# Rewriting the attention stage of a six-stage kernel: its norm inside, query tiles in another order, first maxima beside the projections, products over half rows

## The chip, the cores and the metric

The kernel is one program on one core of a Trainium2 chip. The metric is device time in microseconds (us), the median of several runs of the whole program. Engines are named as in the profile: PE is the TensorE matmul, PEld its weight load, DVE is VectorE, ACT is ScalarE, POOL is GpSimd, SP is the queue that issues the transfers.

## What is computed

Six stages run one after the other on `x` (2 sequences of 512 tokens, width 512), each on a layer norm of `x`: a feed-forward with 4-bit weights, a Mamba-2 block, the same feed-forward again, a routed low-rank block, causal attention, the routed block again.

```python
x = x + 0.5 * _L0_ffn_ref(_layernorm(x), ...)
x = x + _L0_attn_ref(_layernorm(x), ...)
x = x + 0.5 * _L0_ffn_ref(_layernorm(x), ...)
x = x + 0.5 * _L1_ffn_ref(_layernorm(x), ...)
x = x + _L1_attn_ref(_layernorm(x), L1_attn_Wq, L1_attn_Wk, L1_attn_Wv, L1_attn_Wo)
x = x + 0.5 * _L1_ffn_ref(_layernorm(x), ...)
```

The attention has 32 query heads and 8 key heads of size 16; q and k are rotated by cos and sin:

```python
q = _apply_rope(q, cos, sin)
k = jnp.repeat(_apply_rope(k, cos, sin), GROUPS, axis=1)
logits = jnp.where(causal, jnp.einsum('bhqd,bhkd->bhqk', q, k) * scale, lowest)
attn = jax.nn.softmax(logits, axis=-1)
out = jnp.einsum('bhqk,bhkd->bhqd', attn, v)
return out.transpose(0, 2, 1, 3).reshape(bsz, q_len, NH * HD) @ Wo.T
```

## The kernel before

Each stage is a function that writes its own instruction lists, one per engine (`@block.tensor`, `@block.vector` and so on), which run in the order written and wait for each other on semaphores. Between stages all engines meet at a barrier (`Chip.leave`, L52 and L53). PSUM has eight banks of 512 columns, `ps[0]` to `ps[7]`.

The attention stage (`attention`, L830) first calls `norm_transpose` (L100), which makes the normalised, transposed `hT` behind a barrier of its own, while the weights are loaded. Then, for each of the two sequences (b), `project(b, i)` makes nine products: i=0 is k, 1 to 4 are q, 5 to 8 are v. One step later `rotate(b, i-1)` multiplies by the rotation matrix and `rope` (DVE) combines, with ACT taking the high part (`high_part`) and DVE the low part. One step later again `place(b, i-2)` spreads the result over 8 (k) or 4 (q) stacks of 128 rows, each a pair of matmuls into bank `z % 4`, which ACT (even z) or DVE (odd z) copies out (`keep`, L1149 and L1218). A stack holds two heads, one in its upper and one in its lower 64 rows.

The softmax needs each row's maximum before the exponentials. A *step* is one query tile of 128 tokens of one sequence (`STEPS`, 8 of them, tiles 3, 2, 1, 0). `score(s, z)` is one *unit*: two heads' products of a query tile with all its keys, and two additions of the causal mask, into banks 0 and 1 or 2 and 3 by turns (L1020, L1023); `peak(s, z)` is DVE's maximum over it (L1225). 16 units make a step. `turn_maxima(s)` transposes the maxima (L1029), ACT and DVE split them in two parts, and `maxima(s)` on SP writes them by four transfers into spare rows of the stacks, so that the next products have them subtracted. The units of the first two steps stand alone, ahead of the loop; those of step s+2 stand inside step s.

The loop runs over 40 *quads* (step, half of the heads, key tile). In a quad `score_t` makes four transposed products (L1042, and L1044 for the mask on the diagonal) into banks 4 and 5, ACT takes the exponentials (L1162), and one quad later `weigh` multiplies them with v (L1055, four column groups of 32 at once, bank 6). After each half step `turn_out` and `normalize` (L1069, L1238, L1239), after each step `turn_normed`, `take_normed`, `out_product` and `add_out` (L1077, L1174, L1085, L1249) use bank 7.

Of the kernel before, what the change touches and what calls it, by code (L numbers as in the profile page):

```python
# [79 lines left out]

class Chain:
# [16 lines left out]


def norm_transpose(nc, g, name, dst, xn, rms_w=None, var_out=None, sync=None,  # L100
                   pool_end=None, act_start=None):


    x, ps, ident, nhalf = g["x"], g["ps"], g["ident"], g["nhalf"]
    with ExitStack() as ctx:
        c = Chip(nc, ctx, name)
        st = c.sb("st", [P, NT, 6])
        mv = c.sb("mv", [P, NT, 2])
        ve = c.sb("ve", [P, NT])
        rstd = c.sb("rstd", [P, NT])  # L110
        ss = c.sb("ss", [P, NT])
        sq = c.sb("sq", [P, 2, D])
        r2 = c.sb("r2", [P, NT])
        xr = c.sb("xr", [P, NT, D]) if rms_w is not None else xn
        paired = isinstance(dst, Pair)
        xw = c.sb("xw", [P, 2, DT, P]) if rms_w is not None else None
        var_ready, rstd_ready, xn_ready, ss_ready, r2_ready, xr_ready, t_done, t_used, dve, v2, hi_ready, \
            lo_ready = (c.sem(s) for s in ("var_ready", "rstd_ready", "xn_ready", "ss_ready", "r2_ready",
                                           "xr_ready", "t_done", "t_used", "dve", "v2", "hi_ready", "lo_ready"))

        def bank(t):
            return ps[t % 2].rearrange("p (a n) -> p a n", a=DT)

        def cols(t):
            return slice(t * P, (t + 1) * P)

        with nc.Block() as block:
            @block.sync
            def _(e):
                if sync is not None:  # L130
                    sync(e)

            @block.vector
            def _(e):
                ch = Chain(e, dve)
                for t in range(NT):
                    ch.step(e.bn_stats(st[:, t, :], x[:, t, :]))
                ch.wait()
                for t in range(NT):
                    ch.step(e.bn_aggr(mv[:, t, :], st[:, t, :]))  # L140
                ch.wait()
                e.tensor_scalar(ve[:], mv[:, :, 1], EPS, None, ALU.add).then_inc(var_ready, 1)
                e.wait_ge(rstd_ready, 1)
                for t in range(NT):
                    e.tensor_scalar(xn[:, t, :], x[:, t, :], mv[:, t, 0:1], rstd[:, t:t + 1],
                                    ALU.subtract, ALU.mult).then_inc(xn_ready, 1)
                if var_out is not None:
                    e.wait_ge(xn_ready, NT)
                    for t in range(NT):
                        ch.step(e.bn_stats(st[:, t, :], xn[:, t, :]))  # L150
                    ch.wait()
                    for t in range(NT):
                        ch.step(e.bn_aggr(mv[:, t, :], st[:, t, :]))
                    ch.wait()
                    ch.link(e.tensor_copy(var_out[:], mv[:, :, 1]))
                if rms_w is not None:
                    e.wait_ge(xn_ready, NT)
                    for t in range(NT):
                        ch.step(e.tensor_tensor(x[:, t, :], x[:, t, :], xn[:, t, :], ALU.add))
                    e.wait_ge(ss_ready, NT)  # L160
                    e.tensor_scalar(ve[:], ss[:], 1.0 / D, EPS, ALU.mult, ALU.add).then_inc(v2, 1)
                    e.wait_ge(r2_ready, 1)
                    for t in range(NT):
                        e.tensor_scalar(xr[:, t, :], xn[:, t, :], r2[:, t:t + 1], None,
                                        ALU.mult).then_inc(xr_ready, 1)
                    for t in range(NT):
                        e.wait_ge(t_done, t + 1)
                        if t >= 2:
                            e.wait_ge(lo_ready, t - 1)
                        w = rms_w[:, :].unsqueeze(2).to_broadcast([P, DT, P])  # L170
                        e.tensor_tensor(xw[:, t % 2], bank(t), w, ALU.mult).then_inc(t_used, 1)
                elif paired:
                    for t in range(NT):
                        e.wait_ge(hi_ready, t + 1)
                        e.tensor_tensor(dst.lo[:, :, cols(t)], bank(t), dst.hi_read[:, :, cols(t)],
                                        ALU.subtract).then_inc(t_used, 1)

            @block.gpsimd
            def _(e):
                e.wait_ge(var_ready, 1)  # L180
                e.tensor_tensor(rstd[:], ve[:], nhalf[:, 0:NT], ALU.pow).then_inc(rstd_ready, 1)
                if rms_w is not None:
                    e.wait_ge(v2, 1)
# [646 lines left out]
def attention(nc, g, name):  # L830
# [18 lines left out]
    with ExitStack() as ctx:  # L849
# [67 lines left out]
        def units_at(t):  # L917

            s, j, kt = QUADS[t]
            if s + 2 >= NS:  # L920
                return []
# [1406 lines left out]
```

## Time and profile before

| what | value |
|---|---|
| median of 3 runs | 2520.4 us (2519.33 to 2521.07) |
| the profiled execution | 2520.89 us, its span 2519.0 us |
| PE, DVE, ACT, POOL busy over the span | 94%, 66%, 52%, 53% |
| attention with its norm | 2098.9 to 2454.0 us of the span |
| of it the norm | 2098.9 to 2117.5 |
| projections of sequence 0, of sequence 1 | 2117.5 to 2158.4, 2158.4 to 2198 |
| the first two steps' maxima, alone | 2198 to 2238 |
| the loop over quads and its end | 2238 to 2454 |

The busy share is of instructions on an engine, and a busy PE need not be at its peak: its clock is granted at 1.2 or 2.4 GHz (0.5 or 1.0 in the profile), and the same matmuls take twice as long at the lower.

### The profile page before, as it was taken

What the parts mean: (1) busy time and instruction counts of PE and PEld (TensorE: products, weight loads), DVE (VectorE), ACT (ScalarE), POOL (GpSimd) and SP (SyncE); (2) the same over time, 40 slices, a digit from 0 to 9 for tenths busy, and PEclk for the clock granted to TensorE, in tenths of its full rate; (3) what the DMA queues carried; (4) which work ended last, traced back from release to release, by engine and by line L of the source; (5) the groups of instructions that cost most, each with busy time, mean ns of one, the idle gap of its engine ahead of it and who ended that gap; (6) DMA issues with size and microseconds to landing.
All of it is one profiled execution on the core that took longest, in us unless ns stands there. A gap on an engine that the chain in (4) does not pass through costs nothing. (4 is left out here: it accounts for less than half of the span.)

```text
span 2519.0 us, 32506 instructions
## 1 busy us (share of the span) xinstructions
PE 2371.8 (94%) x12122; PEld 1833.6 (73%) x12122; DVE 1661.3 (66%) x2163; ACT 1313.1 (52%) x1902; POOL 1329.8 (53%) x875
## 2 busy tenths in 40 slices
PE   6997899999999999999999999999889986989986
PEld 5876688888888888888888888888668753565643
DVE  5555887687588588588578678678365535674424
ACT  2323576477477467467467567567423223325533
POOL 2221498599499499589579679669622200000000
PEclk9998999999999999999999999999889998989997
DMA  4321333233233233233233323323134202000001
GB/s 128 97 80 46 115 110 105 89 96 119 79 111 115 80 104 103 93 100 114 88 102 109 92 89 117 98 95 102 46 84 97 90 14 78 1 2 2 2 1 47
DMA packets 163260, 203.98 MB, mean 81 GB/s; under 512 B 24380, under 2 KB 86080, under 8 KB 162976
## 3 DMA queue, kind: packets, MB, share of 16 engines
q1 hardware_dynamic: 163104, 201.90, 26.3%
q8 instruction: 98, 1.61, 0.2%
q14 instruction: 58, 0.48, 0.1%
HBM read 198.37 MB, written 3.15 MB: 80 GB/s over the span
## 5 line engine op out<-in xcount | busy, mean ns | idle before, releaser
L1892 POOL TENSOR_TENSOR mamba_w_lo<-mamba_raw,mamba_w_hi 128x512 fp32r<-128x512 f32 x272 | 436.1, 1613 | 289.9 <-ACT mamba_w_hi L1720 289.9
L76 PE MATMUL psum<-mamba_hT_lo,mamba_w_hi 128*128 128x512 f32 x1152 | 461.7, 401 | 5.6 <-DVE mamba_bc L1983 3.0
L77 PE MATMUL psum<-mamba_hT_hi,mamba_w_hi 128*128 128x512 f32 x1152 | 456.2, 396 | 0.0
L78 PE MATMUL psum<-mamba_hT_hi,mamba_w_lo 128*128 128x512 f32 x1152 | 456.1, 396 | 0.0
L1911 POOL TENSOR_SCALAR mamba_L<-mamba_A,mamba_ts 128x256 f32<-128x256 f32 (+1 forms) x256 | 334.3, 1320 | 0.1
L2015 DVE TENSOR_TENSOR mamba_L<-mamba_L,mamba_cb 128x1536 f32<-128x1536 f32 x128 | 302.0, 2359 | 22.2 <-ACT mamba_L L1769 16.5
L76 PEld LDWEIGHTS psum<-mamba_hT_lo,mamba_w_hi 128*128 128x128 f32 x1152 | 217.0, 188 | 55.9 <-DVE mamba_bc L1983 3.3
L1983 DVE SCALAR_TENSOR_TENSOR mamba_hid<-psum,mamba_cw,mamba_hid 128x1022 f32<-128x1022 f32 (+2 forms) x192 | 245.1, 1277 | 18.0 <-ACT mamba_hid L1727 13.5
L78 PEld LDWEIGHTS psum<-mamba_hT_hi,mamba_w_lo 128*128 128x128 f32 x1152 | 216.9, 188 | 52.4
L77 PEld LDWEIGHTS psum<-mamba_hT_hi,mamba_w_hi 128*128 128x128 f32 x1152 | 216.9, 188 | 49.1
L2042 DVE SCALAR_TENSOR_TENSOR mamba_zs_lo<-mamba_z,mamba_dgn,mamba_zs_hi 128x512 fp32r<-128x512 f32 x128 | 117.6, 923 | 172.0 <-ACT mamba_zs_hi L1792 172.0
L395 POOL TENSOR_TENSOR ffn_w_lo<-ffn_deq,ffn_w_hi 128x512 fp32r<-128x512 f32 (+2 forms) x66 | 86.2, 1307 | 262.6 <-ACT ffn_w_hi L405 262.6
L2000 DVE SCALAR_TENSOR_TENSOR mamba_L<-mamba_A,mamba_ts,mamba_zero 128x256 f32<-128x256 f32 (+1 forms) x512 | 214.7, 487 | 1.1 <-DMA mamba_A<-mamba_a_dram 1.1
L76 PE MATMUL psum<-mamba_w_lo,mamba_zs_hi 128*128 128x512 f32 x512 | 205.7, 402 | 10.0 <-DVE mamba_zs_lo L2042 10.0
L78 PE MATMUL psum<-mamba_w_hi,mamba_zs_lo 128*128 128x512 f32 x512 | 203.0, 396 | 0.0
L77 PE MATMUL psum<-mamba_w_hi,mamba_zs_hi 128*128 128x512 f32 x512 | 203.0, 396 | 0.0
L1792 ACT ACTIVATE mamba_zs_hi<-mamba_z,mamba_dgn 128x512 fp32r<-128x512 f32 x128 | 91.7, 722 | 200.2 <-PE psum L78 200.2
L566 POOL MEMSET routed_qT<- 1x1024 f32 x2 | 1.9, 945 | 356.5 <-POOLq L53 356.5
L1727 ACT ACTIVATE mamba_hid<-psum,mamba_cw 128x1024 f32<-128x1024 f32 x64 | 77.3, 1208 | 201.0 <-PE psum L78 201.0
L1720 ACT CAST mamba_w_hi<-mamba_raw 128x512 fp32r<-128x512 f32 x272 | 165.7, 610 | 27.2 <-PE psum L78 25.8
L1574 PE MATMUL psum<-mamba_L,mamba_hc 128*64 128x256 f32 x1024 | 159.4, 390 | 3.6 <-DVE mamba_L L2015 3.6
L2028 DVE SCALAR_TENSOR_TENSOR mamba_z<-mamba_hid,mamba_dgn,psum 128x1024 f32<-128x1024 f32 x64 | 81.9, 1280 | 120.2 <-PE psum L1578 120.2
(278 smaller groups left out, 5002.7 us busy)
## 6 DMA issues: line engine op xcount, KB each, us to landing
mamba_A<-mamba_a_dram SPq DMA_DIRECT2D x128, 512.0 KB, 4.4
mamba_raw<-in_win SPq DMA_DIRECT2D x144, 256.0 KB, 2.6
mamba_raw<-in_wout SPq DMA_DIRECT2D x128, 256.0 KB, 2.6
mamba_Eb<-mamba_e_dram SPq DMA_DIRECT2D x128, 128.0 KB, 3.0
ffn_raw<-in_w SPq DMA_DIRECT2D x80, 128.0 KB, 3.5
ffn_scl<-in_s SPq DMA_DIRECT2D x80, 128.0 KB, 3.7
ffn_scl<-in_s SPq DMA_DIRECT2D x86, 64.0 KB, 2.3
ffn_raw<-in_w SPq DMA_DIRECT2D x20, 256.0 KB, 2.6
```

Source lines behind the costliest of these rows:

```text
L76: e.matmul(out, wh, ml, start=start, stop=False)
L77: e.matmul(out, wh, mh, start=False, stop=False)
L78: return e.matmul(out, wl, mh, start=False, stop=stop)
L1574: e.matmul(psum[lo:lo + HD, 5 + b, q:q + HALF], hc[:, token_tile(b, c, 0), lo:lo + HD], L[:, m % 3, c, h, 0:HALF], start=True, stop=False)
L1720: e.copy(w.hi[:, k % NSPLIT, :], raw[:, k % NRAW, :]).then_inc(s["w_hi"], 1)
L1792: e.activation(zs.hi[:, q % 2, :], z[:, i, p, :], ACT.Copy, scale=dgn[:, grp, i, 1:2]).then_inc(s["z_hi"], 1)
L1892: e.tensor_tensor(w.lo[:, k % NSPLIT, :], raw[:, k % NRAW, :], w.hi_read[:, k % NSPLIT, :], ALU.subtract).then_inc(s["w_lo"], 1)
L1911: last = e.tensor_scalar(out, A[:, m % 2, h, lo:SEQ], ts[:, token_tile(b, 1, j), 1, head], 0.0, ALU.subtract, ALU.min)
L1983: ins = e.scalar_tensor_tensor(t[:, :, k:], banks(kind, n)[:, :, :SEQ - k], cw[:, grp, i, 3 - k:4 - k], t[:, :, k:], ALU.mult, ALU.add)
L2000: last = e.scalar_tensor_tensor(out, A[:, m % 2, h, lo:hi], ts[:, token_tile(b, c, j), 1, head], zero[:, 0:1].to_broadcast([P, hi - lo]), ...
L2015: e.tensor_tensor(t, t, cb[:, m % 2].unsqueeze(2).to_broadcast([P, 2, 2, WCOL]), ALU.mult).then_inc(s["m_ready"], 1)
L2042: e.scalar_tensor_tensor(zs.lo[:, q % 2, :], z[:, i, p, :], dgn[:, grp, i, 1:2], zs.hi_read[:, q % 2, :], ALU.mult, ALU.subtract).then_inc ...
```

## The change

Nearly all of it is in the attention stage.

- `norm_transpose` is gone. Statistics, normalisation and transposes stand in the attention's own lists: tiles 0 to 3, then `project(0, 0)`, then tiles 4 to 7. POOL converts `sel`.
- The steps take the query tiles 1, 2, 3, 0. Units of tile 1 hold two stacks (`DEEP` 2) and those of tile 0 four, so steps 0, 1, 6 and 7 have 8, 8, 4 and 4 units.
- `score` and `score_t` use 64 rows per head in place of 128 with zeros; the two heads of a stack use the two halves of the array. The mask is added from halves too: four matmuls a unit in place of two.
- `score` has banks 0 and 1 alone and waits for the unit before it (`peaked, k`; it was `peaked, k - 1`). `score_t` has banks 2 to 5.
- The eight units of step 0 and two of step 1 stand beside the projections of sequence 1 (`BESIDE`), whose stacks go through banks 2 and 3 alone (`stack_bank`). The other units stand in up to four slots of a quad (`WITHIN`, `SLOTS`): 3 to 4 a quad up to quad 15 (2 in quads 6 and 11), 2 in quads 16 to 25, 1 in 26 to 33.
- All stages get `keep_clock`: transposes of the identity whose result nobody reads, while PE would wait at the start of a stage. The feed-forward takes `hT` rows ahead of the first weights, and the routed block orders `query(1)`, `score(1)` and `pick` earlier.

```diff
+def keep_clock(e, out, ident, n):
+    for _ in range(n):
+        e.transpose(out[:, 0:P], ident[:], ident[:])
...
-    STEPS = [(b, qt) for qt in reversed(range(QT)) for b in range(SEQS)]
+    STEPS = [(b, qt) for qt in (1, 2, 3, 0) for b in range(SEQS)]
...
+    BESIDE = {0: {0: 2, 1: 2, 2: 2, 3: 1, 4: 1}, 1: {7: 1, 8: 1}}
+    WITHIN = {1: {0: 3, 1: 3}, 2: {1: 1, 2: 3, 3: 4, 4: 4, 5: 4}, 3: {6: 2, 7: 3, 8: 3, 9: 3, 10: 3, 11: 2},
...
+        def stack_bank(b, z):
+            return z % 4 if b == 0 else 2 + z % 2
...
                 def score(s, z):
                     b, qt = STEPS[s]
-                    k, n = s * NQ + z, P * (qt + 1)
-                    if k >= 2:
-                        e.wait_ge(peaked, k - 1)
-                    for h in range(2):
-                        e.matmul(psum[:, 2 * (k % 2) + h, 0:n], qs[:, b, z, qt * P:(qt + 1) * P],
-                                 ks[:, b, 2 * (z // QPK) + h, 0:n], start=True, stop=False)
-                    for h in range(2):
-                        last = e.matmul(psum[:, 2 * (k % 2) + h, n - P:n], identr[:], maskr[:], start=False, stop=True)
+                    k, n = UNIT[s, z], P * (qt + 1)
+                    if k:
+                        e.wait_ge(peaked, k)
+                    for y in range(DEEP[s]):
+                        for h in range(2):
+                            e.matmul(psum[:, h, y * n:(y + 1) * n], qs[HALVES[h], b, z + y, qt * P:(qt + 1) * P],
+                                     ks[HALVES[h], b, 2 * ((z + y) // QPK) + h, 0:n], start=y == 0, stop=False)
+                    for j in range(2):
+                        for h in range(2):
+                            out = psum[:, h, 0:DEEP[s] * n].rearrange("p (y n) -> p y n", y=DEEP[s])
+                            last = e.matmul(out[:, :, n - P:n], shifted[HALVES[h], P // 2 * (1 - j):P // 2 * (1 - j) + P],
+                                            halfm[HALVES[h], j, :].unsqueeze(1).to_broadcast([P // 2, DEEP[s], P]),
+                                            start=False, stop=j == 1)
                     last.then_inc(scored, 1)
...
+                for i in range(NV):
+                    ahead, behind = beside(i)
+                    for u in ahead:
+                        score(*u)
+                    project(1, i)
+                    if 1 <= i <= NR:
+                        rotate(1, i - 1)
+                    if 2 <= i <= NR + 1:
+                        place(1, i - 2, behind)
...
                 for t in range(TEND):
+                    if t < TQ:
+                        score_t(t, 0)
+                    for u in unit_in(t, 0):
+                        score(*u)
+                    if t in MAXIMA_AT:
+                        turn_maxima(MAXIMA_AT[t])
+                    if 1 <= t <= TQ:
+                        weigh(t - 1)
+                    for u in unit_in(t, 1):
+                        score(*u)
+                    if t < TQ:
+                        score_t(t, 1)
+                    for u in unit_in(t, 2):
+                        score(*u)
```

On PE, a quad off the diagonal in the first step of before holds two units (L1020 and L1023) between the transposed products (L1042), and then the product with v (L1055):

```order
L1042 MATMUL psum<-attn_qs,attn_ks 128x512 x2
L1020 MATMUL psum<-attn_ks,attn_qs 128x384 x2
L1023 MATMUL psum<-attn_maskr,attn_identr 128x128 x2
L1042 MATMUL psum<-attn_qs,attn_ks 128x512 x2
L1020 MATMUL psum<-attn_ks,attn_qs 128x384 x2
L1023 MATMUL psum<-attn_maskr,attn_identr 128x128 x2
L1055 MATMUL psum<-attn_hT,attn_v 32x512 x4
```

On PE in the changed kernel, the end of quad 3 and the most of quad 4 (L992 and L996 are the transposed products, L964 and L969 a unit, L1008 the product with v):

```order
L996 MATMUL psum<-attn_identr,attn_halfm 128x4x64 x4
L964 MATMUL psum<-attn_ks,attn_qs 128x384 x2
L969 MATMUL psum<-attn_halfm,attn_shifted 128x128 x4
L964 MATMUL psum<-attn_ks,attn_qs 128x384 x2
L969 MATMUL psum<-attn_halfm,attn_shifted 128x128 x4
L992 MATMUL psum<-attn_qs,attn_ks 128x512 x2
L964 MATMUL psum<-attn_ks,attn_qs 128x384 x2
L969 MATMUL psum<-attn_halfm,attn_shifted 128x128 x4
L1008 MATMUL psum<-attn_hT,attn_v 32x512 x4
L964 MATMUL psum<-attn_ks,attn_qs 128x384 x2
L969 MATMUL psum<-attn_halfm,attn_shifted 128x128 x4
L992 MATMUL psum<-attn_qs,attn_ks 128x512 x2
```

Four units stand in a quad where two did, each with four mask matmuls, and between two of them there is at most one other group.

On DVE in the changed kernel, the projections of sequence 1 from the first rope on (L1206 to L1211 are `rope`, L1217 `keep`, L1227 `peak`):

```order
L1206 TENSOR_TENSOR attn_early<-attn_early,attn_cos 128x512
L1208 TENSOR_TENSOR attn_early<-psum,attn_sin 128x512
L1209 TENSOR_TENSOR attn_early<-attn_early 128x512
L1211 TENSOR_TENSOR attn_parts_lo<-attn_early,attn_parts_hi 128x512
L1227 TENSOR_REDUCE attn_mx<-psum 128x2x2 x2
L1206 TENSOR_TENSOR attn_early<-attn_early,attn_cos 128x512
L1208 TENSOR_TENSOR attn_early<-psum,attn_sin 128x512
L1209 TENSOR_TENSOR attn_early<-attn_early 128x512
L1211 TENSOR_TENSOR attn_parts_lo<-attn_early,attn_parts_hi 128x512
L1217 CAST attn_ks<-psum 128x512
L1227 TENSOR_REDUCE attn_mx<-psum 128x2x2
L1217 CAST attn_ks<-psum 128x512 x3
```

Before, this stretch has no reduce: all of them come after the last copy of a stack. Now two stand behind the first rope and one between two copies.

## Rows read from the trace of the kernel before

**Rows 1.** The page: busy time of each engine, and the granted clock in 40 slices.

```profile
PE 2371.8 (94%) x12122; PEld 1833.6 (73%) x12122; DVE 1661.3 (66%) x2163; ACT 1313.1 (52%) x1902; POOL 1329.8 (53%) x875
...
PEclk9998999999999999999999999999889998989997
```

**Rows 2.** Windows: stretch, length, then busy us per engine, granted clock, DMA, GB/s.

```profile
2098.90:2117.50 18.60, 6.91 (x32) 5.41 (x32) 9.82 (x25) 7.64 (x11) 2.36 (x3) 0.63 0.75 262
...
2158.40:2198.00 39.60, 37.17 (x132) 21.86 (x130) 21.04 (x32) 13.40 (x27) 0.00 (x0) 1.00 0.01 1
2198.00:2238.00 40.00, 31.12 (x130) 23.60 (x131) 37.05 (x33) 0.26 (x1) 0.00 (x0) 0.91 0.01 1
2238.00:2454.00 216.00, 199.67 (x1095) 124.09 (x1095) 84.89 (x143) 104.54 (x191) 0.00 (x0) 0.97 0.01 2
```

**Rows 3.** Timeline of the units that stand alone: start us, length us, instruction.

```profile
2201.26 3.48 DVE L1225 TENSOR_REDUCE attn_mx<-psum 128x2 f32<-128x1024 f32 x3
...
2202.53 0.72 PE L1020 MATMUL psum<-attn_ks,attn_qs 128*128 128x512 f32 x2 [0.23 <-DVE attn_mx L1225]
...
2203.09 0.33 PE L1023 MATMUL psum<-attn_maskr,attn_identr 128*128 128x128 f32 x2
```

**Rows 4.** Timeline of one quad of the loop.

```profile
2262.68 0.42 PEld L1020 LDWEIGHTS psum<-attn_ks,attn_qs 128*128 128x128 f32 x2
2262.87 2.28 ACT L1162 ACTIVATE attn_hT<-psum 128x512 f32<-128x512 f32 x4 [1.34 <-PE psum L1042]
...
2263.63 0.96 DVE L1225 TENSOR_REDUCE attn_mx<-psum 128x2 f32<-128x768 f32 x1 [1.22 <-PE psum L1023]
...
2264.97 1.07 PE L1055 MATMUL psum<-attn_hT,attn_v 128*32 128x512 f32 x8
...
2265.96 0.19 PEld L1042 LDWEIGHTS psum<-attn_qs,attn_ks 128*128 128x128 f32 x1 [0.84 <-ACT attn_hT L1162]
```

**Rows 5.** Groups by shape from 2198 to 2454: busy us, mean ns, idle before.

```profile
L1162 ACT ACTIVATE attn_hT<-psum 128x512 f32<-128x512 f32 x160 | 89.3, 596 | 70.5 <-PE psum L1044 42.2 <-PE psum L1042 25.2
...
L1225 DVE TENSOR_REDUCE attn_mx<-psum 128x2 f32<-128x1024 f32 x32 | 36.8, 1218 | 3.6 <-PE psum L1023 3.4
L1085 PE MATMUL psum<-attn_wo,attn_oT 128*128 128x512 f32 x64 | 32.6, 657 | 0.8 <-ACT attn_oT L1174 0.8
L1225 DVE TENSOR_REDUCE attn_mx<-psum 128x2 f32<-128x768 f32 x32 | 30.7, 959 | 25.5 <-PE psum L1023 25.5
```

**Rows 6.** Timeline of `rotate` and `place` of k, sequence 1.

```profile
2169.53 1.02 PE L999 MATMUL psum<-attn_raw,attn_rot 128*128 128x512 f32 x2
...
2172.57 1.07 ACT L1149 CAST attn_ks<-psum 128x512 fp32r<-128x512 f32 x2
...
2173.31 1.28 DVE L1218 CAST attn_ks<-psum 128x512 fp32r<-128x512 f32 x2
...
2175.54 0.59 PE L986 MATMUL psum<-attn_hT,attn_wq 128*128 128x512 f32 x1
```

**Rows 7.** Transfers of the maxima from 2216 to 2245: KB, us to landing.

```profile
attn_qs<-attn_mh SPq DMA_DIRECT2D x4, 8.0 KB, 1.9
```

**Rows 8.** Timeline of a unit at the lower clock.

```profile
2218.50 0.55 PEld L1020 LDWEIGHTS psum<-attn_ks,attn_qs 128*128 128x128 f32 x2
...
2219.57 0.52 PE L1023 MATMUL psum<-attn_maskr,attn_identr 128*128 128x128 f32 x2
```

**Rows 9.** Windows of three short stretches of the attention.

```profile
2213.50:2216.90 3.40, 1.95 (x10) 1.35 (x9) 3.40 (x4) 0.00 (x0) 0.00 (x0) 1.00 0.00 0
...
2271.50:2274.90 3.40, 2.69 (x17) 1.36 (x17) 1.92 (x2) 2.11 (x4) 0.00 (x0) 1.00 0.05 10
...
2442.20:2445.60 3.40, 1.50 (x9) 0.83 (x8) 1.37 (x3) 0.08 (x1) 0.00 (x0) 1.00 0.00 0
```

**Rows 10.** Windows of stretches at the lower clock in other stages.

```profile
2083.80:2090.60 6.80, 5.61 (x10) 2.66 (x11) 4.49 (x14) 5.32 (x15) 0.00 (x0) 0.50 0.00 0
...
1841.40:1858.50 17.10, 9.34 (x30) 7.68 (x31) 13.97 (x32) 3.19 (x6) 4.91 (x4) 0.50 0.51 120
```

More of the change, by code:

```diff
@@ L641, in _ @@
                 score(0)
+                query(1)
+                score(1)
                 e.wait_ge(gelu, 2)
@@ L653, in _ @@
                 e.wait_ge(z1, 1)
+                keep_clock(e, ps[6], ident, 10)
                 turn_weights(1)
@@ L909, in attention @@
         m_in = [c.sem(f"m_in{i}") for i in range(2)]
+        neg_in = [c.sem(f"neg_in{b}") for b in range(SEQS)]
         def stacks_of(n):
@@ new lines, in place @@
+                        if b:
+                            e.wait_ge(kept, STACKS // 2 + z // 2)
+                        elif z >= 4:
+                            e.wait_ge(kept, z // 2 - 1)
+                        s = QPK + z if i == 0 else (z - NKV) % QPK
+                        out = ps[stack_bank(b, z)]
+                        e.matmul(out, sel[:, 0, s, :], parts.hi[:, n % 2, :], start=True, stop=False)
+                        e.matmul(out, sel[:, 1, s, :], parts.lo[:, n % 2, :], start=False, stop=True
+                                 ).then_inc(placed, 1)
@@ new lines, in _ @@
+                e.wait_ge(w_in, 7 * 16)
+                project(0, 0)
+                for t in range(HALF_T, NT):
+                    turn(t)
+                for i in range(1, NV):
+                    project(0, i)
+                    if i <= NR:
+                        rotate(0, i - 1)
+                    if i == 2:
+                        e.wait_ge(sel_ready, 1)
+                    if 2 <= i <= NR + 1:
+                        place(0, i - 2)
+                e.wait_ge(st_act, STACKS // 2)
@@ L1262, in _ @@
-                for t in range(TEND):
+                for h in range(2):
+                    for t in range(h * HALF_T, (h + 1) * HALF_T):
+                        ch.step(e.bn_stats(st[:, t, :], x[:, t, :]))
+                    ch.wait()
+                    for t in range(h * HALF_T, (h + 1) * HALF_T):
+                        ch.step(e.bn_aggr(mv[:, t, :], st[:, t, :]))
+                    ch.wait()
+                    e.tensor_scalar(ve[:, half(h)], mv[:, half(h), 1], EPS, None, ALU.add).then_inc(var_ready, 1)
@@ new lines, in _ @@
+                for t in range(NT):
+                    if t % HALF_T == 0:
+                        e.wait_ge(rstd_ready, t // HALF_T + 1)
+                    if t >= HALF_T:
+                        e.wait_ge(t_done, t - HALF_T + 1)
+                    e.tensor_scalar(xn[:, t % HALF_T, :], x[:, t, :], mv[:, t, 0:1], rstd[:, t:t + 1],
+                                    ALU.subtract, ALU.mult).then_inc(xn_ready, 1)
+                e.wait_ge(w_in, 7 * 16)
+                for i in range(1, NR + 2):
+                    if i <= NR:
+                        rope(0, i - 1)
+                    if i >= 2:
+                        keep(0, i - 2)
@@ new lines, in _ @@
+                for i in range(NV):
+                    ahead, behind = beside(i)
+                    for u in ahead:
+                        peak(*u)
+                    if 1 <= i <= NR:
+                        rope(1, i - 1)
+                    if 2 <= i <= NR + 1:
+                        keep(1, i - 2, behind)
+                        continue
+                    if i == NR + 2:
+                        low_maximum(0)
+                    for u in behind:
+                        peak(*u)
@@ L1267, in _ @@
                             normalize(*of)
-                        elif what == "m":
-                            low_maximum(*of)
-                    for unit in units_at(t) if t < TQ else []:
-                        peak(*unit)
+                    for u in unit_in(t, 3):
+                        peak(*u)
 UNITS = GROUPS * GT
```

456 lines of the change are left out of this document (201 added, 255 removed).

## The prediction

> **What bounds the kernel now.** I read the page first: PE is busy 94% of the span and its clock is near full in all slices but those of the attention [rows 1]. So a gain must take work or idle time off PE, and a new wait of PE is paid in full. The windows of the attention come next [rows 2]. In the norm PE is busy 6.91 of 18.6 us at a clock of 0.63, while the weights land. The projections of sequence 1 keep it busy 37.17 of 39.6 us. In the 40.0 us of the maxima alone DVE is the limit, 37.05 busy. The timeline shows the form of that limit: three reduces run back to back in 3.48 us, and PE starts the next unit when a bank comes free [rows 3]. In the loop PE is busy 199.67 of 216.0 us, with DVE at 84.89 and ACT at 104.54. There it works ahead of the others, because a unit's reduce runs on one pair of banks while PE fills the other. The last of what I read is single quads [rows 4] and the groups by shape [rows 5].
>
> **Stretch of maxima removed.** The 32 units between 2198 and 2238 stand alone no more: -40.0 us [rows 2]. Their work comes back in two places.
>
> **Projections of sequence 1, +23.6 us.** Ten units now stand in them.
> - Their matmuls and the change of the array's shape: a change costs the weight load 0.84 us, as before the next L1042 [rows 4]. Most of it lies under waits for raw and rope; I take 0.8 net for each of the three pairs at i=0, 1, 2: +2.4.
> - The first unit behind `rope` blocks. Its peak stands behind the rope's four DVE instructions, and the next unit on PE waits for that peak, with the projections behind it. Rope and high part take until the copies start, 3.04 (ACT) to 3.78 us (DVE) after `rotate` [rows 6]; a peak takes 1.22 [rows 5]. Together 5.1 us in which PE waits and cannot go on to `project`: +5.1.
> - `place` has two banks, not four. The third stack of k waits for ACT's copy of the first, 3.04 + 0.59 us after `rotate`, the fourth for DVE's copy. Before, the next `project` started 6.0 us after `rotate` [rows 6]; now I reckon 8.6, +2.6. The q stacks wait likewise: +2.4 each at i=3 and 4, where a unit follows, +1.7 for the last two together. In all 9.1; everything on PE is queued behind.
> - At the end two units of step 1, the turning of the maxima (1.1 us), the issue of four transfers on SP (three gaps of 0.62, an estimate from other issues) and 1.9 us to landing [rows 7] lie ahead of `score_t(0, 0)`. Before, other units hid this for step 0. Next to what overlaps: +4.5.
> - These waits let the clock fall once: +2.5.
> Bounds: 8 (only the matmuls and the end) to 32.
>
> **Norm, -1.5 us.** The weights land some 15 us after the stage's start either way, at 262 GB/s [rows 2], so normalising sooner buys little. The second barrier goes, but 16 transposes of tiles 4 to 7 stand behind `project(0, 0)`. The copy of `sel` on POOL is shown by no row here; between 3 and 16 us, by other POOL copies, and hidden by the first two projections up to 8. Bounds -6 to +5.
>
> **Other stages, -14 us.** The starts of the feed-forward and the end of the routed block run at a clock of 0.5: PE busy 9.34 of 17.1 us there, and 5.61 of 6.8 [rows 10]. Those matmuls would take half at full clock, so -2 for each feed-forward and for Mamba, -4 for each routed block, where the reordered queries help as well. Five such places, less one for the transposes that are themselves in the way when the input is early: -14, bounds -6 to -20.
>
> **Loop at full clock, +8 us.** `score` has one pair of banks, so units form a chain over PE and DVE: matmuls, reduce, matmuls. Of a unit before, the load at 2262.68 is followed by its reduce at 2263.63, 0.95 us [rows 4]; with 512 columns the two groups end 0.89 us after the start at 2202.53 [rows 3]. Two halves at once save about 0.23, since the pair takes 0.72 now. That leaves 0.67 to 0.70, and 0.05 from reduce to PE [rows 3]. With the reduces of 959 and 1218 ns [rows 5] the spacing is 1.7 us for units of 768 elements, 2.0 for 1024. Other matmuls between two units (two transposed products, or the product with v at 1.0 with its drain [rows 4]) fit beside the reduce, and so neither cost nor help. Quads 0 to 25 hold 70 units: 38 x 2.0 + 32 x 1.7 = 130 us. To it come 4.4 for products with v beyond the reduce, 13.6 for four out products (32.6 / 8 = 4.1 us each [rows 5], 0.7 of it covered), 1.6 for maxima: 150. Quads 26 to 33 take about 30, 34 to 39 29, the tail 15, at the pace of before. 224 against 216.0 [rows 2]. ACT's four exponentials a quad keep their 596 ns [rows 5] and aren't the limit. Bounds 200 (spacing 1.5) to 240.
>
> The Trainium skill (TensorEngine Tiling (Array Packing), Overview) gives up to twice the throughput for tiles of 64 rows and, in Key Properties, says that changing the tiling mode drains the engine. Alone, the first would take the loop's two kinds of scores to half; the second is the 0.84 us of [rows 4], now more often. By the first alone the sum would be lower by some 40 us, by the second higher by up to 20.
>
> **Clock in the loop, +41 us.** In the chain PE computes some 0.7 of each 1.7 to 2.0 us and less than one other group beside. In this trace stretches in which it had 1.95 of 3.4 and 1.50 of 3.4 us were followed by a fall to 0.5; one with 2.69 of 3.4 was not [rows 9]. Quads 0 to 25 give 2.4 to 3 us of work in 6 to 6.7, like the former. At the lower clock a unit lasts from its load at 2218.50 to 2220.09, 1.6 us [rows 8]; less the half done at once (0.4) and with the reduce, spacing is 2.1 and 2.45. So 38 x 0.45 + 32 x 0.4 = 30 more; the product with v stands beyond the reduce by 0.9 in 25 quads, 23; transposed products in quads of two units 5; quads behind 25 another 5. 63 if the clock stays down. After each out product, eight unbroken matmuls of 657 ns [rows 5], it comes back for a while; I take two thirds of 63. Bounds 0 and 63.
>
> A rule speaks for the same: the Trainium skill (TensorE: Matmul & The Clock Gate, A second HAM failure mode: psum-queue depth-cycling) says short idles between groups make the clock oscillate though data is there. The two falls above agree.
>
> **Sum.** -40.0 + 23.6 - 1.5 - 14 + 8.3 + 41 = +17.4, on the profiled execution's 2520.9: 2538 us. Its time is 0.5 above the median of 2520.4, far below the rest of the uncertainty.
>
> **Rivals.**
> - *The clock stays up, faster.* The chain is as said, but half-row pairs and the work between units are enough to hold 1.0. For it: the stretch with 2.69 of 3.4 kept it. 2538 - 41 = 2497. It is decided in quads 0 to 15: if the granted clock there is above 0.85, it holds, and below 17.4 us of clock cost the kernel isn't slower. 0.24.
> - *The chain isn't the limit.* Reduces start early enough that the loop goes by PE's own work: 199.67 less about half of the scores, near 185 us. For it: before, DVE has 25.5 us idle ahead of the 768 reduces [rows 5], so it was waiting for PE. Against it: `peaked, k`. 2521 - 40 + 24 - 1 - 14 - 31 = 2459. 0.10.
> - *Half-row products don't run side by side.* The two halves, and the four mask matmuls, go one after the other with loads between: 0.25 to 0.45 more on each of 78 units, some 28 us at 0.35: 2566. Nothing in this trace shows 64-row products, only that the product with v, four groups of 32 columns, does eight in 1.07 us [rows 4]. 0.14.
>
> The Trainium skill (TensorE: Matmul & The Clock Gate, Part 3) measures 3.07 times, not 4, for four row tiles; that lies between the forecast and the last rival.
>
> **How the numbers follow.** The forecast has 0.52, its own range 2515 to 2560. 0.2% of the time, 5 us, is about what a measurement of this kernel tells from no change. Faster by more: both first rivals (0.34) and the forecast's low tail (0.05), 0.39. Within: 0.08, from the forecast and the upper side of the first rival. Slower: 0.39 of the forecast and the last rival's 0.14, 0.53. The range 2466 to 2566 leaves out most of the second rival and the upper half of the last, about 0.18.
>
> **What would show it.** In the changed profile: no stretch with DVE alone between projections and loop; projections of sequence 1 at 63 us with idle of PE ended by DVE's `keep` and `peak` and ACT's copies; reduces (L1227) spaced 1.7 and 2.0 us where the clock is up, 2.1 and 2.45 where it isn't; a loop of about 265 us whose granted clock is between 0.6 and 0.8 up to quad 25, with idle of PE ended by DVE `attn_mx`; clocks near 1.0 at the starts of the other stages. The prediction is wrong if the reduces are nearer than 1.6 us to each other, if the loop's clock stays near 1.0, or if the stall at i=2 is absent.

## The result, and the profile after

The changed kernel takes 2502.27 us (median of 4 runs, 2500.2 to 2507.46), the kernel before 2520.31 on the same chip: 0.9934 of it, 95% interval 0.992 to 0.9948. It is 18 us faster, where 17 us slower was forecast. The profiled execution took 2504.12 us, 16.8 less than that of before.

The page of the changed kernel, as [rows 1]:

```profile
PE 2365.6 (95%) x12542; PEld 1814.6 (73%) x12542; DVE 1656.7 (66%) x2124; ACT 1307.3 (52%) x1903; POOL 1333.4 (53%) x878
...
PEclk9999999999999999999999999999899998978999
```

The windows of its attention, which answer to [rows 2]: the norm, the projections of sequence 1 with ten units beside them, quads 0 to 25, the rest of the loop with its end, and the whole loop. Columns: stretch, length, busy us of PE, PEld, DVE, ACT, POOL, granted clock, DMA share, GB/s.

```profile
2089.80:2105.00 15.20, 8.31 (x42) 7.54 (x42) 9.95 (x26) 3.34 (x8) 6.19 (x7) 0.72 0.88 324
2148.50:2210.40 61.90, 48.91 (x212) 27.15 (x212) 33.19 (x43) 14.18 (x28) 0.00 (x0) 0.97 0.01 2
2210.40:2371.40 161.00, 137.08 (x911) 76.76 (x911) 86.42 (x97) 65.21 (x123) 0.00 (x0) 0.81 0.01 2
2371.40:2439.80 68.40, 59.17 (x393) 27.73 (x392) 17.21 (x29) 35.05 (x68) 0.00 (x0) 0.98 0.01 2
2210.40:2439.80 229.40, 196.25 (x1303) 104.50 (x1303) 103.64 (x125) 100.26 (x191) 0.00 (x0) 0.86 0.01 2
```

Where the time went, beside the terms of the prediction:

| part | forecast | profiled executions |
|---|---|---|
| stretch of maxima alone | -40.0 | 40.0 to none: -40.0 |
| projections of sequence 1 | +23.6 | 39.7 to 61.9: +22.2 |
| norm and projections of sequence 0 | -1.5 | 59.5 to 58.7: -0.8 |
| other stages | -14 | -12.5 (feed-forwards -3.1 and -1.8, Mamba -1.0, routed -3.1 and -3.5) |
| loop | +8.3 and +41 | 215.0 to 229.4: +14.4 |
| sum | +17.4 | -16.7 |

Four terms of five are within 1.5 us of what was measured. All but a little of the error stands in the loop.

Reduces of units in the changed kernel (timeline of DVE: start, length, instruction, idle before it and what ended it), first at full clock, in quad 8, then at the low one, in quad 5:

```profile
2273.43 0.96 DVE L1227 TENSOR_REDUCE attn_mx<-psum 128x2 f32<-128x768 f32 x1 [0.71 <-PE psum L969]
2275.09 0.96 DVE L1227 TENSOR_REDUCE attn_mx<-psum 128x2 f32<-128x768 f32 x1 [0.71 <-PE psum L969]
2276.76 0.96 DVE L1227 TENSOR_REDUCE attn_mx<-psum 128x2 f32<-128x768 f32 x1 [0.71 <-PE psum L969]
...
2249.39 0.96 DVE L1227 TENSOR_REDUCE attn_mx<-psum 128x2 f32<-128x768 f32 x1 [0.31 <-PE psum L969]
2251.45 0.96 DVE L1227 TENSOR_REDUCE attn_mx<-psum 128x2 f32<-128x768 f32 x1 [1.11 <-PE psum L969]
```

They come 1.67 us apart with 0.71 idle between, and 2.07 at the low clock: forecast were 1.7 and 2.1. (With 1024 elements the closest at the low clock come 2.44 apart, at full clock most come 1.99 apart, against 2.45 and 2.0.) The chain through one pair of banks is there as described.

The PE side of it shows what the chain leaves room for (timeline of PE, quad 8):

```profile
2274.44 0.44 PE L964 MATMUL psum<-attn_ks,attn_qs 64*128 64x384 f32 x2 [0.77 <-DVE attn_mx L1227]
2274.72 0.33 PE L969 MATMUL psum<-attn_halfm,attn_shifted 64*128 64x128 f32 x4
...
2274.98 1.07 PE L1008 MATMUL psum<-attn_hT,attn_v 128*32 128x512 f32 x8
...
2276.11 0.44 PE L964 MATMUL psum<-attn_ks,attn_qs 64*128 64x384 f32 x2
```

Two halves of a product stand as one row of 0.44 us, side by side. The product with v fits between two units: of the 1.67 us from one to the next PE is busy 0.61 with the unit and 1.07 with that product.

In the projections, the wait behind the first rope and one wait of `place` (timeline of PE):

```profile
2160.01 0.50 PE L964 MATMUL psum<-attn_ks,attn_qs 64*128 64x256 f32 x4
...
2164.10 0.50 PE L964 MATMUL psum<-attn_ks,attn_qs 64*128 64x256 f32 x4 [3.35 <-DVE attn_mx L1227]
...
2185.38 0.50 PE L950 MATMUL psum<-attn_parts_hi,attn_sel 128*128 128x512 f32 x1 [1.05 <-ACT attn_qs L1133]
```

### The profile page after: what moved, and what is told of

The parts are those of the page before. It is cut to its first block and busy times, and to the rows that moved or that the text cites. A ratio compares the mean times of both kernels' runs of the same rounds, so it can differ in the third digit from the quotient of the medians.

```text
span 2502.3 us, 33261 instructions
## 1 busy us (share of the span) xinstructions
PE 2365.6 (95%) x12542; PEld 1814.6 (73%) x12542; DVE 1656.7 (66%) x2124; ACT 1307.3 (52%) x1903; POOL 1333.4 (53%) x878
## 5 line engine op out<-in xcount | busy, mean ns | idle before, releaser
L2053 DVE TENSOR_TENSOR mamba_L<-mamba_L,mamba_cb 128x1536 f32<-128x1536 f32 x128 | 302.0, 2359 | 22.2 <-ACT mamba_L L1807 16.4
```

The source lines that it names most:

```text
L2053: e.tensor_tensor(t, t, cb[:, m % 2].unsqueeze(2).to_broadcast([P, 2, 2, WCOL]), ALU.mult).then_inc(s["m_ready"], 1)
```

## The experiments

Each kernel was timed beside the kernel before on the same chip; ratios are to that. The changed kernel has 0.9934. "Quads 0 to 25" is read from the first transposed product to the product with v of quad 25, "low" the time at the granted clock of 0.5 in the loop, 65 us in the changed kernel.

### e1: work for PE where it waits

```diff
+    HOLD = (3, 0, 3, 6)
...
+                def hold(t, slot):
+                    if turns_at(t) or t in MAXIMA_AT or slot == 0 and turns_at(t - 1):
+                        return
+                    for u in unit_in(t, slot)[:1]:
+                        wait_spare()
+                        keep_clock(e, ps[7], ident, HOLD[slot])
```

> The changed kernel with transposes of the identity (three, or six between two units in a row) into bank 7 ahead of units of the loop, where bank 7 is free, so that PE computes while it would wait for the reduce. In the changed kernel's trace the clock is low for 61 us of the first 110 us of the loop, and a unit is then spaced 2.07 or 2.44 us in place of 1.67 or 1.99. Theory A (low clock costs only the PE part of each link of the chain, about a fifth of the time it lasts): with the clock held the time falls by 8 to 13 us, the loop from 229 to about 218. Theory B, the one in the prediction (low clock is dear, 41 us of the loop): a fall of over 25 us. Theory C (the transposes delay the units as much as they help): no change within 3 us, with the clock at 1.0 and spacings over 1.8 for units of 768 elements.

0.9911 (0.9892 to 0.993), 2496.23 us. The loop has 31 us at the low clock, and quads 0 to 25 took 155.7 in place of 161.0. By the ratios that is 6 us less than the changed kernel, under the 8 to 13 of theory A, and the two intervals overlap. The direction is theory A's, and a fall of over 25 us is out; but the added transposes also delayed some quads (quad 19 took 4.74 in place of 4.07), so the price of the clock was not settled by it.

### e2: two pairs of banks for units

```diff
-                        e.wait_ge(peaked, k)
+                        e.wait_ge(peaked, k - 1 if k >= ALONE else k)
...
-                        e.wait_ge(exped, 2 * k - 2)
+                        e.wait_ge(exped, 2 * k)
...
-                    outs = [ps[2 + 2 * (k % 2) + h].rearrange("p (h q) -> p h q", h=QPK) for h in range(2)]
+                    outs = [ps[4 + h].rearrange("p (h q) -> p h q", h=QPK) for h in range(2)]
```

`ALONE` is 10, the units beside the projections; from there on units write to banks 0 and 1 or 2 and 3 by turns.

> The changed kernel with two pairs of banks for the units of the loop (0 and 1, 2 and 3 by turns, each unit waits for the unit before the last) and one pair, 4 and 5, for the transposed products, each of which then waits for both exponentials of the one before. Theory A (the chain of matmuls and reduce through one pair of banks sets quads 0 to 25): reduces come 1.25 to 1.5 us apart in place of 1.67 and 1.99, a quad of four units takes 5 to 5.5 us in place of 6.7, quads 26 and on 0.3 us more each; the time falls by 20 to 35 us. Rival (PE's own work or the exponentials set the quads, the wait for the reduce is only where the slack shows): within 5 us of the changed kernel.

0.9814 (0.9796 to 0.9832), 2472.07 us. Windows of its quads 0 to 25 and of the rest, and its reduces (timeline of DVE):

```profile
2214.75:2332.66 117.91, 107.65 (x911) 64.61 (x911) 83.70 (x97) 64.98 (x123) 0.00 (x0) 0.99 0.01 2
2332.66:2408.63 75.97, 59.11 (x393) 27.22 (x392) 17.87 (x29) 35.70 (x69) 0.00 (x0) 1.00 0.01 2
```

```profile
2229.02 0.96 DVE L1233 TENSOR_REDUCE attn_mx<-psum 128x2 f32<-128x768 f32 x1
2230.57 3.55 DVE L1233 TENSOR_REDUCE attn_mx<-psum 128x2 f32<-128x768 f32 x4 [0.58 <-PE psum L975]
```

118 us in place of 161, with the same instructions: four reduces back to back in 3.55 us. The clock stayed at full, low for 3 us. Split at the start of quad 16, the changed kernel first, then e2:

```profile
2210.40:2323.83 113.43, 94.80 (x600) 54.78 (x601) 57.74 (x67) 40.04 (x75) 0.00 (x0) 0.73 0.01 2
2323.83:2368.60 44.77, 40.53 (x298) 21.01 (x299) 27.37 (x29) 23.47 (x45) 0.00 (x0) 1.00 0.01 2
```

```profile
2214.75:2288.10 73.35, 67.47 (x601) 42.30 (x601) 55.03 (x67) 39.59 (x75) 0.00 (x0) 0.98 0.01 3
2288.10:2331.11 43.01, 38.63 (x299) 21.29 (x299) 28.08 (x30) 24.38 (x46) 0.00 (x0) 1.00 0.01 2
```

So the chain did set quads 0 to 15, which the rival denied: 73 us in place of 113. Quads 16 to 25, with two units each, gained 2 us only: there the loads of units waited 7.7 us for reduces in the changed kernel, and in e2 the loads of transposed products wait 14.2 us for the exponentials. These, now with one pair of banks, also made the rest 76 in place of 68. The 43 us are the banks and the clock together: PE, waiting less, kept the full clock. At the price found below, 0.27 to 0.32 a us, 58 us fewer at the low clock are 16 to 19 of them.

### e3 and e9: full rows

e3 takes the products of a unit over 128 rows, where the other head's are zeros:

```diff
-                            e.matmul(psum[:, h, y * n:(y + 1) * n], qs[HALVES[h], b, z + y, qt * P:(qt + 1) * P],
-                                     ks[HALVES[h], b, 2 * ((z + y) // QPK) + h, 0:n], start=y == 0, stop=False)
+                            e.matmul(psum[:, h, y * n:(y + 1) * n], qs[:, b, z + y, qt * P:(qt + 1) * P],
+                                     ks[:, b, 2 * ((z + y) // QPK) + h, 0:n], start=y == 0, stop=False)
```

> The changed kernel with the units' products over 128 rows of stacks (the other head's rows are zeros), one after the other, in place of two over 64 rows each; masks as changed. Theory A (the two half-row products of a unit run side by side, and the saved pass lies on the chain): each unit's spacing grows by one pass, 0.16 us at 384 columns and 0.21 at 512, at full clock: 78 units, +13 to +17 us, more if the clock falls more, less if the added work holds it. Rival (halves run one after the other anyway): no change within 3 us. Second rival (longer work of PE holds the clock, which pays for the longer links): between -5 and +5 with the granted clock of the loop above 0.93.

1.0117 (1.0098 to 1.0135), 2548.05 us: 46 us more than the changed kernel, three times what theory A said. Spacings were 2.04 and 2.43, and a unit shows why (timeline of PE's load):

```profile
2273.29 0.30 PEld L964 LDWEIGHTS psum<-attn_ks,attn_qs 128*128 128x128 f32 x2 [1.09 <-DVE attn_mx L1227]
...
2273.83 0.30 PEld L969 LDWEIGHTS psum<-attn_halfm,attn_shifted 64*128 64x128 f32 x4 [0.25 <-issue]
```

The load of the half-row masks waited 0.25 us behind full-row products, for nothing that the profile shows. e9 gives the masks full rows too, and two of them:

```diff
-                            last = e.matmul(out[:, :, n - P:n], shifted[HALVES[h], P // 2 * (1 - j):P // 2 * (1 - j) + P],
-                                            halfm[HALVES[h], j, :].unsqueeze(1).to_broadcast([P // 2, DEEP[s], P]),
-                                            start=False, stop=j == 1)
...
+                        last = e.matmul(out[:, :, n - P:n], identr[:], maskr[:].unsqueeze(1).to_broadcast(
+                            [P, DEEP[s], P]), start=False, stop=True)
```

> The kernel of full rows (e3), with the mask of a unit added by two products over 128 rows in place of four over 64. In e3 units came 2.04 and 2.43 us apart in place of 1.67 and 1.99, though one pass is 0.16 and 0.21, and PE's weight load waited 0.25 between the unit's products and its masks. Theory A (half of that price is the change between 128 and 64 rows within a unit): spacings 1.85 to 1.95 and 2.2 to 2.3, quads 0 to 25 176 to 183 us, 8 to 16 us less than e3. Rival (the price lies in passes and loads that follow one another, not in the change): spacings within 0.05 of e3.

1.0003 (0.9994 to 1.0013), 2520.63 us. Spacings 1.84 and 2.22, quads 0 to 25 168.5 us in place of e3's 193.6. Theory A's direction holds, but by the ratios e9 takes 29 us less than e3, where it had 8 to 16; part of that is the clock, low for 24 us of these quads in place of 55. With one kind of rows in a unit, the halves are worth 0.17 us on a unit of 384 columns and 0.23 on one of 512; mixing both kinds costs another 0.2. In e9 the load of the masks follows that of the products without a gap:

```profile
2251.67 0.30 PEld L965 LDWEIGHTS psum<-attn_ks,attn_qs 128*128 128x128 f32 x2 [0.94 <-DVE attn_mx L1228]
2251.95 0.36 PEld L969 LDWEIGHTS psum<-attn_maskr,attn_identr 128*128 128x128 f32 x2
```

The Trainium skill (TensorEngine Tiling (Array Packing), Key Properties) says that changing the tiling mode drains the engine; these traces agree, with 0.25 us before the load in e3 and none in e9.

### e4: without the transposes of the identity

```diff
-    for _ in range(n):
+    for _ in range(0 * n):
```

> The changed kernel without any of the added transposes of the identity, in all stages; the reordered instructions stay. The other stages took 12.8 us less than before the change in the profiled executions. Theory A (most of that is the clock at the starts of the stages): +9 to +14 us, with the clock at 0.5 at the starts of the feed-forward and in the routed block. Rival (the reordering in the feed-forward and routed block gives most of it): +1 to +5 us.

0.9955 (0.9937 to 0.9974), 2510.05 us, 5 us more than the changed kernel by the ratios, whose intervals overlap a little; the stages of the profiled executions show more. The profiled routed blocks took 51.8 and 51.8 us (50.9 and 52.1 in the changed kernel, 53.9 and 55.6 before), the feed-forwards 201.5 and 202.3 (199.2 and 200.3; 202.3 and 202.1 before). So the routed block gains by its order, the feed-forward by the clock; neither theory had it whole.

### e5, e11 and e6: the ten units alone

e5 has the ten units between projections and loop, and four banks for the stacks of both sequences; e11 is e5 with two banks for the stacks of sequence 1; e6 is e5 with two pairs of banks for units, and from quad 26 on two pairs for transposed products.

```diff
-            return z % 4 if b == 0 else 2 + z % 2
+            return z % 4
...
-            return units[:-1], units[-1:]
+            return [], []
```

```diff
+            return 2 * ((k - ALONE + 1) % 2) if ALONE <= k < LATE else 0
+
+        def pair_t(t, m):
+            return 2 if t >= TLATE and m else 4
```

(The first piece is e5's, the second e6's, where `ALONE` is 1, `LATE` 80 and `TLATE` 26.)

> The changed kernel with no unit beside the projections of sequence 1: the ten units stand between projections and loop, through their one pair of banks, and the stacks of both sequences go through four banks again. Theory A (what the units and the two banks for stacks cost the projections, 22.2 us in the trace, is about what ten units cost alone): projections of sequence 1 back to 40 us, ten units with the maxima's way to the stacks 21 to 23 us behind them; the time within 4 us of the changed kernel. Rival (placing units beside projections is where the change gains): +10 us or more.

> The kernel of e5 (ten units between projections and loop) with the stacks of sequence 1 through two banks, as in the changed kernel. Theory A (of the 22 us that the projections of sequence 1 grew by, 9 are the two banks, as the prediction reckons): the projections take 47 to 50 us in place of 39.2. Rival (the two banks hardly matter, since place waits for rope anyway): under 42 us.

> The ten units between projections and loop as before it, two pairs of banks for units from the first on, and from quad 26 on, where a quad has one unit or none, two pairs for the transposed products and one for the units. Theory A: units alone come every 1.14 us, so projections and ten units take 40 + 16 in place of 62; quads 0 to 25 take 118 as with two pairs, and from quad 26 on 68 in place of 75. In all 12 to 14 us less than with two pairs of banks alone, 2458 to 2461. Rival (without work of projections beside them, units let the clock fall, and the loop starts at the low clock): over 2466.

The windows of e5, projections of sequence 1 and then ten units with the way of the maxima, and of e11's projections:

```profile
2150.43:2189.64 39.21, 37.20 (x132) 21.90 (x130) 21.04 (x32) 13.11 (x26) 0.00 (x0) 1.00 0.01 1
2189.64:2214.32 24.68, 11.58 (x82) 8.63 (x81) 12.01 (x11) 0.52 (x2) 0.00 (x0) 0.57 0.01 2
```

```profile
2149.87:2199.05 49.18, 41.12 (x132) 22.21 (x130) 21.50 (x32) 13.72 (x26) 0.00 (x0) 0.97 0.00 1
```

e5 took 0.996 (0.9945 to 0.9975), 63.9 us for the two stretches where the changed kernel took 61.9. Placing the units beside the projections is worth 2 us in the trace and about 6.5 by the ratios, two measurements with different other stages; the ten units and two banks cost the projections nearly what the units cost alone. e11 took 0.9991 (0.9981 to 1.0): two banks make the projections 10.0 us longer, against 9.1 in the prediction. e6 took 0.9757 (0.974 to 0.9773), 2456.74 us: projections and units 54.5 us, quads 0 to 25 118.9, the rest 70.1. It is the fastest kind here, 61 us under the kernel before by the ratio, and the clock of its loop was low for 9 us only.

### e7, e8 and e12

e7 is e2 with e6's banks from quad 26 on. e8 moves the unit at i=1 ahead of `rotate` and its reduce ahead of the rope:

```diff
+                    if i == 1:
+                        for u in behind:
+                            score(*u)
+                        behind = []
                     if 1 <= i <= NR:
                         rotate(1, i - 1)
```

e12 is e6 with `keep_clock(e, ps[6], ident, 12)` ahead of the loop.

> Two pairs of banks for the units of the loop up to quad 25, from quad 26 on two pairs for the transposed products and one for the units; ten units beside the projections as in the changed kernel. Theory A (transposed products that wait for the exponentials of the ones before made quads 26 to 39 6.8 us longer with two pairs of banks for units): 5 to 7 us less than with two pairs throughout, 2465 to 2467. Rival (the tail's length has another cause, such as the clock): no change.

> The changed kernel with one unit moved: the unit at i=1 of the projections of sequence 1 stands ahead of rotate on PE, and its reduce ahead of the rope on DVE. Theory A (the next unit waits 3.35 us for a reduce that stands behind the rope's four instructions): that wait goes to under 1.3 us, the projections of sequence 1 take 2 to 4 us less. Rival (rope, high part and the copies are the chain of this stretch, and rope now starts later by the reduce): the wait is gone, but place waits as much longer, no change within 1.5 us.

> The kernel of e6 with twelve transposes of the identity ahead of the loop, where PE waits some 2.5 us for the maxima. Theory A (the clock falls there): 8.7 us at the low clock in the loop go, and 1 to 2 us of time: 2455 to 2457. Rival: no change, or the transposes delay the first transposed product by up to 1 us.

e7: 0.9793 (0.9779 to 0.9808), 2465.8 us, the rest of the loop 70.3 us in place of e2's 76.0, which agrees with theory A. e8: from the first product of k to the loop it took 56.7 us, where the changed kernel takes 61.2, a little more than theory A had; the whole gave 0.9945 (0.9928 to 0.9962), which doesn't show it, as it lies within the spread of the other stages. e12: 0.9752 (0.9738 to 0.9767). No low clock is left in its loop. Its whole time, 2457.24 us, can't be told from e6's; the traces have its loop at 185.5 us, where e6's takes 188.9, so the last 9 us at the low clock were worth some 3 there.

### e10 and e13: the price of the low clock

e10 is e1 with transposes ahead of the units of every quad and of the loop. e13 has fourteen ahead of the loop, and in the loop only those in quads 0 to 6 and 11 to 14 where bank 7 isn't in use:

```diff
+                    if 6 < t < 11 or t > 14 or slot == 0 and turns_at(t - 1) or slot == 3 and turns_at(t):
+                        return
```

> The kernel of e1 with transposes of the identity ahead of the units of every quad (one behind the product with v), and twelve ahead of the loop, where PE waits for the maxima. e1 had quads 0 to 25 in 155.7 us with some 27 us of them at the low clock, the changed kernel 161.0 with 61. Theory A (low clock costs 0.15 us of each us that it lasts): under 12 us at the low clock, quads 0 to 25 in 151 to 154 us. Rival (what e1 gained was not the clock, or the transposes now delay the units): 156 us or more though the clock is full.

> The changed kernel with fourteen transposes of the identity ahead of the loop and with three, two or four ahead of units in quads 0 to 6 and 11 to 14 alone, where the clock fell in the changed kernel's trace, and only where bank 7 is not in use, so that the others are not delayed. Two accounts of what the low clock cost the loop are open. By quads: quad 13 takes 5.98 us at full clock in one trace and 7.75 in four others of the same loop, quad 2 5.78 and 8.40, so about 0.28 of each us at the low clock, 17 us in all: then quads 0 to 25 take 144 to 150 us here, with under 15 us at the low clock, and the time falls by 9 to 15 us. By e1 and e10: the gain was 5 us for 35 us fewer at the low clock, and at full clock quads 0 to 25 took even longer (171 us): then 155 us or more here, though the clock is full.

e10 gave 1.0008 (0.9998 to 1.0018), e13 0.9891 (0.9875 to 0.9908), 2492.89 us. Windows of quads 0 to 25, first e10, then e13:

```profile
2210.73:2381.66 170.93, 150.22 (x1109) 84.93 (x1109) 86.25 (x97) 65.62 (x123) 0.00 (x0) 0.99 0.01 2
```

```profile
2209.58:2357.70 148.12, 124.21 (x960) 69.58 (x960) 86.26 (x97) 65.11 (x123) 0.00 (x0) 0.99 0.01 2
```

Both have the full clock but for 3.4 us. In e10 the transposes wait for bank 7 and stand before units that could have gone: 171 us. (Their weight loads wait 9.2 us for DVE's `attn_on`, which reads that bank, in nine waits.) In e13 quads 0 to 25 take 148.1, 12.9 less than in the changed kernel, with 58 us fewer at the low clock, and by the ratios the whole takes 11 us less. The account by quads holds; that of e1 and e10 was their own delay. The 12.9 us are a lower bound for what the low clock cost, since e13's transposes delay some quads too (quad 11 took 3.70 in place of 3.14). The same quad at both clocks, with the same instructions: quad 13 in the changed kernel, then in e5:

```profile
2300.16:2307.91 7.75, 6.58 (x44) 3.86 (x42) 3.68 (x3) 2.17 (x4) 0.00 (x0) 0.57 0.01 2
```

```profile
2304.92:2310.89 5.97, 4.03 (x42) 2.42 (x42) 3.68 (x3) 2.17 (x4) 0.00 (x0) 1.00 0.01 3
```

1.78 us more with 6.7 us at the low clock: 0.27 for each. Quad 2 in the changed kernel, then in e1, where it has no added transposes and the same instructions:

```profile
2225.85:2234.25 8.40, 7.13 (x39) 3.83 (x38) 3.99 (x5) 3.01 (x6) 0.00 (x0) 0.52 0.02 5
```

```profile
2229.60:2235.38 5.78, 4.24 (x41) 2.34 (x39) 3.55 (x5) 3.02 (x6) 0.00 (x0) 1.00 0.02 6
```

2.62 us more with 8.1 at the low clock: 0.32 for each. Over the 61 us at the low clock in quads 0 to 25 that is an estimate of 16 to 20 us.

## Why the prediction was wrong

**The step that failed is the clock in the loop, +41.** Its price a us was right: 63 us more over some 213 is 0.30 for each us at the low clock, and quads 13 and 2 show 0.27 and 0.32. Wrong was how long it would last. Two thirds of quads 0 to 25 were to be at the low clock, some 140 us; it was 61, which cost 16 to 20 us in place of 41. The sentence that failed is "Quads 0 to 25 give 2.4 to 3 us of work in 6 to 6.7, like the former". By its size the work there was reckoned in passes of columns (the prediction doesn't show the sum), and set against rows that give PE's busy time in the profile [rows 9], in which every matmul counts with its whole length: quad 8, at full clock, has PE busy 4.08 of 5.69 us. Read in the same measure, the changed kernel has this (windows):

```profile
2209.10:2212.50 3.40, 0.97 (x10) 0.78 (x10) 1.83 (x2) 1.08 (x2) 0.00 (x0) 1.00 0.02 3
2222.70:2226.10 3.40, 1.60 (x18) 1.12 (x16) 1.86 (x3) 1.09 (x2) 0.00 (x0) 1.00 0.02 5
2239.80:2243.20 3.40, 1.91 (x19) 1.22 (x22) 1.97 (x3) 1.09 (x2) 0.00 (x0) 1.00 0.00 0
...
2273.90:2277.30 3.40, 2.50 (x22) 1.21 (x22) 1.98 (x3) 1.74 (x4) 0.00 (x0) 1.00 0.00 0
...
2297.80:2301.20 3.40, 2.00 (x20) 1.35 (x20) 2.06 (x2) 1.41 (x3) 0.00 (x0) 1.00 0.04 10
```

The clock fell behind the four with 0.97, 1.60, 1.91 and 2.00, and not behind the one with 2.50, nor behind six others read between 2270 and 2354, with 2.36 to 3.09. The stretches of [rows 9] show the same: falls behind 1.95 and 1.50, none behind 2.69. A quad with three units has its transposed products and the product with v between them, and PE is busy some 2.5 of 3.4 us; it was less at the loop's start, where PE waits for the maxima, and at the ends of quads 1, 3 and 12, where one unit follows another with nothing or little between. PE's busy time alone doesn't part the two kinds, though: in the kernel before, the clock also fell behind 2.18 of 3.4 us, and in the changed kernel it stayed up behind 2.16, in quads 34 and 35. What decides between them is not shown. The two windows:

```profile
2234.00:2237.40 3.40, 2.18 (x11) 1.54 (x9) 3.40 (x4) 0.00 (x0) 0.00 (x0) 1.00 0.00 0
```

```profile
2400.20:2403.60 3.40, 2.16 (x17) 0.84 (x17) 0.28 (x1) 2.90 (x7) 0.00 (x0) 1.00 0.01 2
```

The rule that the Trainium skill has for such idles (TensorE: Matmul & The Clock Gate, A second HAM failure mode: psum-queue depth-cycling) describes what was seen, a clock that went down and up four times in quads 0 to 25, but it does not say how much of the time is lost.

**The chain, +8.3.** The mechanism was right to 0.03 us of spacing. At full clock quads 0 to 25 come to some 141 to 145 (161 less 16 to 20; e13's 148 has the cost of its transposes in it), where 150 stood, and the rest to 68 where 74 stood: its pace isn't that of before. The transposed products have four banks, and e2, with two, has 76; what their half rows add was not tried apart. So at full clock the loop would be 2 to 6 us shorter than before (215.0), and not 8 longer. This is the smaller part of the loop's error of 35 us: 11 to 15, beside 21 to 25 for the clock.

**Which rival.** The first, in which the chain is as said and the clock stays up: 2497 against 2502. Its time came close by errors that cancel, not by its mechanism: the clock didn't stay up (granted 0.73 in quads 0 to 15, where it was to be above 0.85), and the 16 to 20 us that this cost were nearly made good by 11 to 15 less in chain and tail. Its second clause, that below 17.4 us of clock cost the kernel isn't slower, can't be decided with a cost of 16 to 20. "The chain isn't the limit" is refuted by e2 for quads 0 to 15 (73 us in place of 113, of which 16 to 19 are clock), and "half-row products don't run side by side" by e3 and e9.

**Projections, +23.6.** 22.2 measured. The two banks cost 10.0 (e11) where 9.1 stood. The wait behind the rope was 3.35 where 5.1 stood (5.04 from the start of `rotate` to the next unit, but PE works in the first part of it), and moving the unit took 4.5 off the stretch (e8). The 0.84 us that the prediction reads in [rows 4] as a change of the array's shape is a wait that ACT's exponentials ended, as the row says; the change itself is 0.25 in e3. What stands at the first pair of units is the chain's own wait (timeline of PE):

```profile
2154.84 0.51 PE L964 MATMUL psum<-attn_ks,attn_qs 64*128 64x256 f32 x4 [1.32 <-DVE attn_mx L1227]
```

That the other parts, with the end, make up the rest was not tried apart. **Norm** -0.8 and **other stages** -12.5 are within the bounds; the split between clock and order in the latter was reckoned otherwise than e4 shows.

**Not separated.** What the new order of query tiles is worth was not tried alone. It lets ten units, not 32, lie ahead of the loop, and the price of that in the loop is the 70 units that it has to take in its first 26 quads.

## What to carry to other kernels

Before a plan is compared with stretches of a profile, put both in the same measure: busy time as the profile counts it, not passes worked out from columns. A producer and a consumer that share one buffer make a chain of the sum of both; here a second pair of banks was worth 30 us, more than the 18 that the change gave, and part of it was the clock that PE kept by waiting less. And work added to hold a clock pays only where the clock falls and nothing waits behind it: placed everywhere it took back more than it gave.

## What was not expected of the hardware

- Mixing row shapes within a short group costs more than the rows: 128-row products followed by 64-row masks made each unit 0.20 to 0.21 us longer than 128-row masks did; the load waits 0.25 us at the change.
- The low clock is cheaper here than its ratio of two: 0.27 to 0.32 us for each us in which it lasts. The reduce takes 0.96 us at both clocks, over half of a link of 1.67.
- A clock that falls or doesn't can hang on little: quad 13, with the same instructions, ran at full clock in one trace of that loop (e5) and mostly at the low clock in four (the changed kernel's, e4, e8 and e11).
